# Scaling the softmax reciprocals by 2^15: on VectorE behind the reciprocal, where ScalarE did it ahead of its own use

## The reference, cut to what matters

```python
xn = _layernorm(x, axis=-1)
qkv = jnp.einsum('bsd,ed->bse', xn, w_qkv) + b_qkv
scores = jnp.einsum('bhqd,bhkd->bhqk', q, k) / math.sqrt(Hd) + causal
attn = jax.nn.softmax(scores, axis=-1)
out = jnp.einsum('bhqk,bhkd->bhqd', attn, v)
attn_out = jnp.einsum('bsd,ed->bse', out, w_out) + b_out
g = jnp.einsum('th,ih->ti', xf, gate_w) * gate_s
u = jnp.einsum('th,ih->ti', xf, up_w) * up_s
ffn = jnp.einsum('ti,hi->th', jax.nn.silu(g) * u, down_w) * down_s
x = x + attn_out + ffn
```

## Time and profile before

| | us |
|---|---|
| median of 3 runs | 1963.78 |
| lowest, highest | 1961.55, 1965.11 |
| the profiled execution, its own time | 1963.78 |
| its span in the profile | 1961.4 |

### The profile page before, as it was taken

How to read it: one execution, slowest core, us unless ns; L and a number is a source line. 1 busy time by engine, 2 the same in 40 slices (tenths; PEclk the granted TensorE clock), 3 DMA queues, 4 the chain that set the end, 5 groups by cost and what they waited for, 6 DMA issues and landing times.

```text
span 1961.4 us, 43852 instructions
## 1 busy us (share of the span) xinstructions
PE 1871.4 (95%) x14978; PEld 1221.6 (62%) x14978; DVE 1565.8 (80%) x4692; ACT 1402.4 (71%) x4104; POOL 1132.0 (58%) x1624
## 2 busy tenths in 40 slices
PE   6689999999999999999999999999999999999996
PEld 4456675666656666566666766666566666756663
DVE  5778888887877878878788888887878778788885
ACT  4767777867767677686776777677776776777674
POOL 4665656647566475665756565464655656565352
PEclk9899999999999999999999999999999999999998
DMA  7997978788797797978879787896968778786784
GB/s 215 231 163 143 190 138 185 147 158 178 127 192 128 162 173 131 199 140 158 166 140 192 136 182 133 158 165 125 191 127 167 146 136 183 133 183 126 129 157 94
DMA packets 818837, 310.24 MB, mean 158 GB/s; under 512 B 756464, under 2 KB 789232, under 8 KB 818608
## 3 DMA queue, kind: packets, MB, share of 16 engines
q1 hardware_dynamic: 800928, 249.44, 70.5%
q0 software_dynamic: 17680, 57.95, 10.6%
HBM read 55.59 MB, written 16.78 MB: 37 GB/s over the span
## 4 chain that ended last, share of the span: by engine, by line
PE 62%; DVE 16%; DMA 6%; SPq 6%; ACT 5%; issue 3%; POOL 2%; DVEq 0%; POOLq 0%; ACTq 0%
PE bank L287 62%; DMA pt<-phl 5%; DVE phl L589 5%; SPq L929 4%; DVE bank L579 3%; ACT phl L483 3%; DVE fh L601 2%; DVE res L613 1%; ACT bank L491 1%; SPq L936 1%; DVE ft L597 1%; DVE small L553 1%; DVE xhl L725 1%; DVE xs L563 1%; ACT small L479 1%
## 5 line engine op out<-in xcount | busy, mean ns | idle before, releaser
L589 DVE SCALAR_TENSOR_TENSOR phl<-bank,small,phl 128x512 f16<-128x512 f32 (+3 forms) x1024 | 525.4, 544 | 157.6 <-ACT phl L483 156.2
L491 ACT ACTIVATE bank<-bank,small 128x512 f32<-128x512 f32 (+3 forms) x1024 | 514.8, 503 | 169.8 <-DVE small L579 167.7
L579 DVE CUSTOM_DVE_ANT_0 bank<-bank,mask 128x512 f32<-128x512 f32 (+3 forms) x1024 | 483.6, 504 | 139.5 <-PE bank L287 137.2
L483 ACT ACTIVATE phl<-bank,small 128x512 f16<-128x512 f32 (+3 forms) x1024 | 500.2, 531 | 109.5 <-DMA pt<-phl 98.4
L790 POOL TENSOR_SCALAR ht<-fh 128x256 f16<-128x256 f32 x352 | 142.5, 405 | 410.3 <-DVE fh L601 409.8
L287 PE MATMUL bank<-xnT,wg 128*128 128x256 f16 x2816 | 367.8, 273 | 7.0 <-DVE fh L601 5.1
L287 PE MATMUL bank<-xnT,wu 128*128 128x256 f16 x2816 | 367.3, 274 | 0.0
L287 PE MATMUL bank<-xnT,wqkv 128*128 128x512 f16 x1536 | 352.1, 379 | 2.1 <-ACT q L452 2.1
L287 PE MATMUL bank<-wd,ht 128*128 128x512 f16 x1408 | 320.2, 384 | 4.1 <-ACT wd L430 3.6
L287 PEld LDWEIGHTS bank<-xnT,wg 128*128 128x128 f16 x2816 | 263.6, 98 | 69.5 <-issue 5.6
L287 PEld LDWEIGHTS bank<-xnT,wu 128*128 128x128 f16 x2816 | 276.8, 98 | 33.1
(11 more groups left out here) (108 smaller groups left out, 2024.9 us busy)
## 6 DMA issues: line engine op xcount, KB each, us to landing
stk<-qkp SPq DMA_DIRECT2D x768, 64.0 KB, 2.1
res<-in_x_dram POOLq DMA_DIRECT2D x64, 256.0 KB, 4.8
xin<-in_x_dram POOLq DMA_DIRECT2D x60, 256.0 KB, 4.5
out_dram<-res POOLq DMA_DIRECT2D x60, 256.0 KB, 3.9
pt<-phl SPq DMA_TRANSPOSE x512, 4.3
xin<-in_gate_dram POOLq DMA_DIRECT2D x11, 256.0 KB, 3.8
xin<-in_up_dram POOLq DMA_DIRECT2D x11, 256.0 KB, 3.7
xin<-in_down_dram POOLq DMA_DIRECT2D x11, 256.0 KB, 3.6
```

Source lines behind the costliest of these rows:

```text
L483: i = eng.activation(phl[qt][:, j % 2, 0], pb[:, off:off + W], ACT.Copy, scale=st_r[:, c:c + 1])
L491: i = eng.activation(pb[:, off:off + W], pb[:, off:off + W], ACT.Exp, bias=st_m[:, c:c + 1], scale=-1.0, accum_out=st_s[:, c:c + 1])
L579: i = eng.tensor_tensor_reduce(out=bk[:, off:off + W], in0=bk[:, off:off + W], in1=mask[:, 512 - W:512], scale=-(32.0 ** -0.5) / (QS * QS) ...
L589: i = eng.scalar_tensor_tensor(phl[qt][:, j % 2, 1], pb[:, off:off + W], st_r[:, c:c + 1], phl[qt][:, j % 2, 0], ALU.mult, ALU.subtract)
```

## The change

The multiplication of the reciprocals by PS moves from ScalarE to VectorE. It stands directly behind the reciprocal, and waits for it on a semaphore, since it reads what the reciprocal has just written. ScalarE's `high` waits for the new semaphore v_rec; a_rec is gone.

```diff
@@ high(n), ScalarE
             for j, qt, off in segs(u):
                 w.wait_ge(d_pt[qt], 16 * (2 * G + j // 2))
-            if n % 2 == 0:
-                c0 = 2 * (n % NSTAT)
-                w.wait_ge(v_rc, n // 2 + 1)
-                eng.activation(st_r[:, c0:c0 + 4], st_r[:, c0:c0 + 4], ACT.Copy, scale=PS).then_inc(a_rec, 1)
-            w.wait_ge(a_rec, n // 2 + 1)
+            w.wait_ge(v_rec, n // 2 + 1)
             for k, (j, qt, off) in enumerate(segs(u)):
@@ reciprocals(n), VectorE
             w.wait_ge(a_exp, n + 2)
             eng.reciprocal(st_r[:, c0:c0 + 4], st_s[:, c0:c0 + 4]).then_inc(v_rc, 1)
+            w.wait_ge(v_rc, n // 2 + 1)
+            eng.tensor_scalar(st_r[:, c0:c0 + 4], st_r[:, c0:c0 + 4], PS, None, op0=ALU.mult).then_inc(v_rec, 1)
```

More of the change, by code:

```diff
@@ L116, in fast_path @@
     s_s, s_qk, s_v, s_av, s_o, s_gu, s_dn, s_oe, s_flag = (sem("s_" + n) for n in ("s", "qk", "v", "av", "o", "gu", "dn", "oe", "flag"))
-    a_exp, a_rec, a_hi, a_q32, a_vh, a_a32, a_ft, a_xh, a_w, a_wo, a_ms = (sem("a_" + n) for n in ("exp", "rec", "hi", "q32", "vh", "a32", "ft", "xh", "w", "wo", "ms"))
-    v_max, v_rc, v_lo, v_fa, v_fh, v_vl, v_oy, v_dd = (sem("v_" + n) for n in ("max", "rc", "lo", "fa", "fh", "vl", "oy", "dd"))
+    a_exp, a_hi, a_q32, a_vh, a_a32, a_ft, a_xh, a_w, a_wo, a_ms = (sem("a_" + n) for n in ("exp", "hi", "q32", "vh", "a32", "ft", "xh", "w", "wo", "ms"))
+    v_max, v_rc, v_rec, v_lo, v_fa, v_fh, v_vl, v_oy, v_dd = (sem("v_" + n) for n in ("max", "rc", "rec", "lo", "fa", "fh", "vl", "oy", "dd"))
     v_bn, v_bna, v_var, v_xs, v_xl, v_w, v_wo, v_peak, v_most, v_chk, v_end = (
```

## The result

| | median us | lowest to highest | runs |
|---|---|---|---|
| before, run beside it | 1964.44 | 1961.55 to 1965.82 | 4 |
| changed | 1983.57 | 1983.32 to 1984.18 | 4 |

The ratio is 1.0097, with a 95% interval of 1.0084 to 1.0110. The change makes the kernel 19.1 us slower. The forecast was 1965.2 us and its range ended at 1973, so the prediction is wrong.

A forecast was written before the change was run, and what follows sets the result against it. The prediction took TensorE, busy 95%, to set most of the time and costed 65 chain places: 3.2 - 2.2 - 1.2 + 1.6 = +1.4 us on 1963.8, so 1965.2 us. Its range for 8 in 10 was 1957.5 to 1973.

The forecast's parts named there:

- What bounds the kernel: Whole span: TensorE, busy 95%, sets most of the time; 60 of 320 reciprocals lie on the chain of waits.
- VectorE, reciprocal to maximum, +0.19 us: At 17 chain places the next maximum starts 0.28 us after the reciprocal's start instead of 0.09: +3.2 us in all.
- ScalarE, reciprocal to high, -0.05 us: At 43 chain places high starts 0.40 us after the reciprocal's start instead of 0.45: -2.2 us in all.
- The new instruction beside GpSimd, 1.6 us: VectorE's added multiplication is held by GpSimd's TENSOR_TENSOR at 11 of 60 chain reciprocals, for 1.6 us together.
- upper bound of 5.0 us: Most that GpSimd's holds could add: L563's mean delay of 0.083 us at each of the 60 chain reciprocals.
- a longest duration near 0.4 us: Sign in the later profile that the port matters: VectorE's new instruction lasts up to about 0.4 us beside GpSimd.
- the other 260: Reciprocals off the chain of waits, said to lie beside longer work, mostly matmuls, and given no cost.
- GpSimd holds the new instruction: Slower rival: L563's mean delay on VectorE applies at the chain's reciprocals, 5.0 us, giving 1968.6 us; chance 0.15.
- VectorE is late behind every reciprocal: Slower rival: idle time before low is too short, so +0.19 us at all 60 chain places, 1975.6 us; chance 0.11.
- ScalarE's relief reaches the end: Faster rival: without L479, ScalarE's queue moves up 0.23 us in 13 pairs of units, 1957.4 us; chance 0.13.

The follow-up runs named there:

- The run with SCALAR_TENSOR_TENSOR: Changed kernel with the same VectorE multiplication issued as a SCALAR_TENSOR_TENSOR with one input in PSUM: 1963.28 us, ratio 0.9991 to the kernel before.
- three reciprocals: Changed kernel with the multiplication replaced by two more reciprocals, each waiting for the one before: 1987.07 us, ratio 1.0103 to the kernel before.

## Why the prediction was wrong, point by point

*What bounds the kernel.* This was right as far as it went: TensorE sets most of the time, and 60 reciprocals lay on the chain. By the same counting the removal of L479 alone should give 43 x 0.24 + 5 x 0.23 = 11.5 us, and 13.2 us (medians) to 16.1 us (ratio) were measured. Here the chain was a fair lower estimate of what a step is worth.

*VectorE, reciprocal to maximum, +0.19 us.* This was right for an instruction that is not held. In the timeline above the one at 1024.42 starts 0.04 us after the reciprocal's end, lasts 0.17, and the maximum starts 0.28 us after the reciprocal, exactly the step that was summed up. The run with SCALAR_TENSOR_TENSOR has the same 0.28.

*ScalarE, reciprocal to high, -0.05 us.* This was right in size for the unheld form: 0.45 us by the median against 0.50.

*The new instruction beside GpSimd, 1.6 us.* This is the step that failed. The mechanism was named and its size was wrong, both in the term and in its upper bound of 5.0 us. The runs price it directly: between the held and the unheld form of the same multiplication in the same place lie 1.0097 and 0.9991, about 1.1% or 21 us, where the term had 1.6. I read off L563 that it was held for 0.29 us, because it took 0.83 in place of 0.54 us, and concluded that GpSimd lets go 0.25 us before its recorded end. The new instruction's rows say that the hold lasts to the end. Then the row of L563 has to be read otherwise: a held instruction does part of its work while it waits, so a long one is late by less than it was held. This reading was not tested by itself. In the earlier trace rows, where L792 ends at 1025.83, L563 still needed 0.28 us after that, out of the 0.54 it takes alone. The instruction of four elements needs 0.02 to 0.04 us after that, out of the 0.17 it takes alone, and so its whole duration is the rest of GpSimd's instruction and hardly more. For L563 alone the two readings give the same times, so only a short instruction could tell them apart, and there was none of this kind in the kernel before. I expected a longest duration near 0.4 us, and it is 1.208. I also let only GpSimd's TENSOR_TENSORs hold it; L788 does so too. Laid over the same 60 places of the trace before, a hold to the end of any GpSimd instruction would have hit 34 in place of 11 and given 6.6 us in place of 1.6. The rest comes with the new order: with the 0.203 us per instruction that the changed kernel shows, the term at 60 places is 12.2 us, and the sum 3.2 - 2.2 - 1.2 + 12.2 = +12.0 us, 1975.8 us: slower by 0.6%, outside the range that I gave.

The Trainium skill's rule ("SBUF — State Buffer", "Who interferes with whom"), that whoever comes first holds the shared port pair for its whole instruction, was right in the strict reading that I had put aside for the row of L563. Here the trace agrees with it in the 249 and the 71 instructions counted above; it does not quite show who comes first, since an L559 that starts 0.03 us ahead of L768 is held. The unheld forms agree with its list of what takes the pair: the RECIPROCAL and the SCALAR_TENSOR_TENSOR with one input in PSUM never do.

*The other 7 us.* The sum priced the change at the places that were critical before. With 0.4 us more in front of every second maximum, more places became critical: 121 reciprocals on the chain in place of 60, VectorE's share 31% in place of 16%. I had written that the other 260 lie beside work that takes longer, and had not asked by how much. That these places make up the 7 us is argued and not shown: three reciprocals have 116 on the chain and cost as much, but SCALAR_TENSOR_TENSOR has 92 and costs nothing.

*The rivals.* "GpSimd holds the new instruction" was the right mechanism with a price of 4.8 us, since it took L563's mean lateness of 0.083 us where the hold is 0.203. "VectorE is late behind every reciprocal" decided at an added 0.23 us; the changed kernel adds 0.40 by the median, and VectorE's idle time in front of `low` did shrink by 88 us. But it shrank by 84 us with SCALAR_TENSOR_TENSOR too, at no cost. Whether there is a threshold on the way to the maximum the runs can hardly tell: a cost in proportion and a cost beyond 0.23 us alone differ by under 0.3% for the unheld forms, which is about the width of their intervals on either side. On the way to `high` the cost is about in proportion, from 0.25 us less (-0.82%) to 0.64 us more (1.86%). "ScalarE's relief reaches the end" is real too, about 0.8% by itself, and more than the 0.33% that I gave it. The change gives it back, since `high` then waits for VectorE's multiplication instead.

## What to carry to other kernels

A short VectorE instruction of the kind that GpSimd can hold costs not its own length but what is left of GpSimd's instruction. Where GpSimd is busy half the time, give it a form that is not held (here one input in PSUM; single columns were not held either, but four of them cost 0.62%) or leave the work where it is. Price a wait by the delay that it puts on the way between two engines as well as by the busy time of the engine: here 0.1 us on the way from the reciprocal to `high` cost two to three times as much as 0.1 us of VectorE in front of the maximum. And the cheapest form of the scaling was none: the kernel with the constant 1 is the fastest, at 0.9918 of the time before. It leaves out what the scaling is there for, keeping the low parts out of float16's lowest range.

## What the runs showed of the hardware

- A four-element TENSOR_SCALAR on VectorE, SBUF to SBUF, lasted 0.169 to 1.208 us, and in 233 of the 234 places where it took over 0.2 us it ended 0.02 to 0.04 us after the GpSimd instruction that ran when it started. In the 71 places where GpSimd ran nothing at its start it took at most 0.172 us. That the instruction is short does not help it.
- TENSOR_SCALAR of one column (1280 of them, 0.142 to 0.156 us), RECIPROCAL of four (0.163 to 0.180 us) and SCALAR_TENSOR_TENSOR of four with one input in PSUM (0.157 to 0.160 us) were held nowhere.
- The record of a held 512-element TENSOR_SCALAR (0.83 us where it takes 0.54 alone) ends 0.28 us after GpSimd's instruction; if the hold ends with that, as for the four elements, its duration shows 0.29 us of a hold of 0.54.
- In 15 of 60 places of the changed kernel the 512-element TENSOR_SCALAR starts 0.03 to 0.04 us ahead of a GpSimd instruction and is held until 0.28 us after that one's end (0.95 to 1.48 us). The four-element one at 1024.42 starts 0.07 us ahead of L790 and is not held.
